# Node and segment products from split float32r operands, with the low part of x formed by VectorE

## The reference

```
neighbor_sum = segment_sum(x[col], row);  deg = max(segment_sum(1, row), 1)
mean = neighbor_sum / deg
h_mean = (x + mean) * 0.5 @ W_mean + b_mean
h_ego  = x @ W_ego + b_ego;   h_nb = mean @ W_nb + b_nb
gate = sigmoid(gw * node_vec + gb)
h = layernorm(x + (1 - gate) * h_mean + gate * concat(h_ego, h_nb))
```

## Time and profile before

| | us |
|---|---|
| median of 3 runs | 2945.29 |
| lowest and highest of them | 2940.87, 7257.4 |
| the profiled execution's own time | 2944.66 |
| its span, first to last instruction | 2942.9 |
| TensorE busy | 2697.9 |
| VectorE busy | 2329.0 |
| ScalarE busy | 1851.3 |
| GpSimd busy | 1582.4 |

### The profile page before, as it was taken

The page is one execution under the profiler, slowest core; times in us unless marked ns, Lnnn a source line. Parts: engine busy times, 40 slices in busy tenths (PEclk is TensorE's granted clock), DMA queues, the critical chain, the costliest instruction groups (busy, mean ns, idle before and its releaser), DMA issues. The chain is left out here.

```text
span 2942.9 us, 52181 instructions
## 1 busy us (share of the span) xinstructions
PE 2697.9 (92%) x13617; PEld 1554.7 (53%) x13617; DVE 2329.0 (79%) x7668; ACT 1851.3 (63%) x3839; POOL 1582.4 (54%) x1491
## 2 busy tenths in 40 slices
PE   4789889999999959999999999999999999976774
PEld 2455556666666525555555555555555555543442
DVE  8777775655565668888888888888888888878996
ACT  2344445555555437777777777777777777757885
POOL 0476717676666375455455454454554554405776
PEclk8799999999999979999999999999999999999998
DMA  9999995565555478777777787777777777647994
GB/s 339 304 301 314 306 308 182 187 192 180 182 189 189 143 182 218 215 223 214 213 227 214 213 221 216 215 218 217 219 217 212 226 213 212 193 118 241 278 278 154
DMA packets 544632, 653.46 MB, mean 222 GB/s; under 512 B 244302, under 2 KB 451850, under 8 KB 544518
## 3 DMA queue, kind: packets, MB, share of 16 engines
q1 hardware_dynamic: 468486, 440.38, 51.6%
q0 software_dynamic: 69472, 208.99, 22.7%
q10 hardware_dynamic: 6560, 2.84, 0.4%
HBM read 315.65 MB, written 299.10 MB: 209 GB/s over the span
## 5 line engine op out<-in xcount | busy, mean ns | idle before, releaser
L942 PE MATMUL bank<-w_node,xT 128*128 128x384 f32 x1564 | 568.5, 501 | 47.2 <-ACT bank L576 46.9
L1219 ACT ACTIVATE hidT<-bank,b1c 128x512 f32<-128x512 f32 x490 | 336.8, 687 | 414.5 <-PE bank L1509 340.7
L1128 POOL TENSOR_TENSOR u_hc<-u_hc 128x1536 f32<-128x1536 f32 x98 | 270.2, 2757 | 551.0 <-issue 429.0
L1509 PE MATMUL bank<-xh,w1h 128*128 128x512 f16 x1568 | 469.8, 381 | 23.1 <-DMA xh<-eh 15.7
L1509 PE MATMUL bank<-xl,w1h 128*128 128x512 f16 x1568 | 468.2, 380 | 0.0
L1509 PE MATMUL bank<-xh,w1l 128*128 128x512 f16 x1568 | 468.2, 380 | 0.0
L942 PEld LDWEIGHTS bank<-w_node,xT 128*128 128x128 f32 x1564 | 291.4, 195 | 227.7 <-ACT bank L576 61.6
L576 ACT ACTIVATE bank<-bias_all 128x512 f32<-128x512 f32 x391 | 234.3, 599 | 267.4 <-DVE H L680 266.2
L1525 PE MATMUL bank<-hidT,w2f 128*64 128x256 f32 x3136 | 360.1, 382 | 0.8 <-ACT hidT L1219 0.8
L1350 DVE STREAM_TRANSPOSE feat<-catT 32x256 f32<-32x256 f32 x784 | 342.5, 437 | 17.0 <-ACT catT L1228 2.4
L673 DVE SCALAR_TENSOR_TENSOR H<-bank,gates,X 128x256 f32<-128x256 f32 x391 | 187.2, 479 | 175.1 <-PE bank L942 172.5
(11 more groups left out here) (248 smaller groups left out, 4833.0 us busy)
## 6 DMA issues: line engine op xcount, KB each, us to landing
hc_tab<-H SPq DMA_DIRECT2D x78, 680.0 KB, 7.9
er<-edge_tab SPq DMA_DIRECT2D x98, 512.0 KB
X<-in_x SPq DMA_DIRECT2D x78, 640.0 KB, 4.8
h_row<-hc_tab SPq DMA_DIRECT2D x97, 512.0 KB
out_x<-o_row SPq DMA_DIRECT2D x97, 512.0 KB, 5.0
hc_tab<-zero_row SPq DMA_DIRECT2D x35, 1344.0 KB, 8.4
edge_tab<-u_x SPq DMA_DIRECT2D x98, 256.0 KB
edge_tab<-feat SPq DMA_DIRECT2D x98, 256.0 KB
```

Source lines behind the costliest of these rows:

```text
L942: ins = t_.matmul(p[:, 0:384], xT[t // 2 % XR][:, t % 2, c * P:(c + 1) * P], w_node[:, c, :], start=False, stop=c == 1, skip_group_check=True)
L1128: g.tensor_tensor(c, c, u_hc[s][:, :, MULT:MULT + 3].unsqueeze(3).to_broadcast([P, 4, 3, P]), ALU.mult).then_inc(u_scaled, 1)
L1219: a.activation(hidT[m][:, :], bank[2 + m % 2][:, :], ACT.Relu, bias=b1c[:, m:m + 1])\
L1509: ins = t_.matmul(bank[2 + m % 2][:, :], w[:, c, m * P:(m + 1) * P], xx[s][:, :, :].rearrange("p (k c) e -> p c k e", c=2)[:, c, :, :], st ...
```

## The change

1. `product` from the pair SPLIT = SUMS // 2 + 1 = 98 on (slot 196 and later): ScalarE copies the transposed x to `xhigh`, in float32r, VectorE subtracts that from bank 0 and gets `xlow` (`low_x`), and TensorE forms high x high, high x low and low x high with the two parts of `w_node`: six float32r matmuls in place of two fp32 ones. `xhigh` and `xlow` have two buffers each. The next `turn` waits for `x_low`.
2. `product_sum` for all pairs the same way: `accT` in float32r, `accL` by VectorE (`low_sum`, in the slot of the copy), six matmuls; the next `turn_sum` waits for `low_out`.
3. The weights are split once, by VectorE, before the loop.
4. Four x buffers in place of three, three H buffers in place of two, the store of a half is issued ahead of its clear. The clears after the fourth take 6.5 tile columns on average in place of 7, so that they end with half 40 in place of half 38.
5. SUMS 188 to 195, SPAN 186 to 177, FIX 378 to 377. `carry` is copied to a tile of its own, `carryT`.

The diff, cut to its core:

```diff
-        CLEARS = (0, 60, 88, 116) + tuple(range(144, NT, 7)) + (NT,)
+        CLEARS = (0, 60, 88, 116) + tuple(144 + 13 * c // 2 for c in range(38)) + (NT,)
...
-        XB = 3
+        XB = 4
...
+                st.done(v.tensor_copy(w_nbh[:, :, :], w_nb[:, :, :]))
+                st.done(v.tensor_copy(w_nodeh[:, :, :], w_node[:, :, :]))
+                st.wait()
+                st.done(v.tensor_tensor(w_nodel[:, :, :], w_node[:, :, :], w_nodeh[:, :, :].bitcast(F32),
+                                        ALU.subtract))
+                st.done(v.tensor_tensor(w_nbl[:, :, :], w_nb[:, :, :], w_nbh[:, :, :].bitcast(F32), ALU.subtract))
...
-        H = [tmp(f"H{s}", [P, HALF, HU]) for s in range(2)]
-        XR = 4
+        HR = 3
+        H = [tmp(f"H{r}", [P, HALF, HU]) for r in range(HR)]
+        XR = 3
...
+        XS = 2
+        xlow = [tmp(f"xlow{b}", [P, 2, D], F32R) for b in range(XS)]
+        xhigh = [tmp(f"xhigh{b}", [P, 2, D], F32R) for b in range(XS)]
...
-        SORT, PHASES, DECODE, SUMS, SPAN, FIX = 0, 7, 16, 188, 186, 378
+        SORT, PHASES, DECODE, SUMS, SPAN, FIX = 0, 7, 16, 195, 177, 377
+        SPLIT = SUMS // 2 + 1
...
+                def half(h):
+                    if h + XB <= 2 * ITER:
+                        load(h + XB)
+                    store(h)
+                    if h < len(CLEARS) - 2:
+                        clear(h + 1)
...
+                    if p >= SPLIT + XS:
+                        act.wait_ge(p_ready, 2 * (p - XS) + 2)
+                    to = xT[p % XR] if p < SPLIT else xhigh[p % XS]
+                    a.activation(to[:, 0:many, :], bank[0][:, 0:many * D].rearrange("p (t d) -> p t d", t=many),
...
+                def low_x(p):
+                    many = min(2, NT + 1 - 2 * p)
+                    dve.wait_ge(xt_copied, p + 1)
+                    if p >= SPLIT + XS:
+                        dve.wait_ge(p_ready, 2 * (p - XS) + 2)
+                    v.tensor_tensor(xlow[p % XS][:, 0:many, :],
+                                    bank[0][:, 0:many * D].rearrange("p (t d) -> p t d", t=many),
+                                    xhigh[p % XS][:, 0:many, :].bitcast(F32), ALU.subtract).then_inc(x_low, 1)
+
+                def low_sum(p):
+                    dve.wait_ge(turned_out, p + 1)
+                    if p >= AR:
+                        dve.wait_ge(prod_ready, 2 * (p - AR) + 2)
+                    v.tensor_tensor(accL[p % AR][:, :, :], bank[4][:, :].rearrange("p (t d) -> p t d", t=2),
+                                    accT[p % AR][:, :, :].bitcast(F32), ALU.subtract).then_inc(low_out, 1)
...
+                    if now % 2 == 0 and SPLIT <= (now + LEAD_X) // 2 <= NT // 2:
+                        low_x((now + LEAD_X) // 2)
+                    for p in tiles_of(now, LATE):
+                        if p < PAIRS:
+                            low_sum(p)
...
                 def turn(p):
-                    if p:
+                    if p > SPLIT:
+                        pe.wait_ge(x_low, p - SPLIT)
+                    elif p:
                         pe.wait_ge(xt_copied, p)
...
+                    if pair >= SPLIT:
+                        pe.wait_ge(x_low, pair - SPLIT + 1)
+                        high, low = xhigh[pair % XS][:, t % 2, :], xlow[pair % XS][:, t % 2, :]
+                        n = 0
+                        for c in range(2):
+                            for part_, w in ((high, w_nodeh), (high, w_nodel), (low, w_nodeh)):
+                                n += 1
+                                ins = t_.matmul(p[:, 0:384], part_[:, c * P:(c + 1) * P], w[:, c, :], start=False,
+                                                stop=n == 6, skip_group_check=True)
...
                     if p:
-                        pe.wait_ge(turned_out, p)
+                        pe.wait_ge(low_out, p)
...
+                        for part_, w in ((accT, w_nbh), (accT, w_nbl), (accL, w_nbh)):
+                            ins = t_.matmul(bank[PRODS[t % 3]][:, 0:U],
+                                            part_[t // 2 % AR][:, t % 2, c * P:(c + 1) * P], w[:, c, :],
+                                            start=n == 0, stop=n == 5)
```

More of the change, by code:

```diff
@@ L144, in build @@
         w_node = sb("w_node", [P, 2, 384])
+        w_nodeh, w_nodel = sb("w_nodeh", [P, 2, 384], F32R), sb("w_nodel", [P, 2, 384], F32R)
         w_nb = sb("w_nb", [P, 2, 384])
+        w_nbh, w_nbl = sb("w_nbh", [P, 2, 384], F32R), sb("w_nbl", [P, 2, 384], F32R)
         w1f = sb("w1f", [P, 2, HEADS * HID])
@@ L376, in build @@
         TEN = 2 * HALF
-        H = [tmp(f"H{s}", [P, HALF, HU]) for s in range(2)]
-        XR = 4
+        HR = 3
+        H = [tmp(f"H{r}", [P, HALF, HU]) for r in range(HR)]
+        XR = 3
         xT = [tmp(f"xT{b}", [P, 2, D]) for b in range(XR)]
+        XS = 2
+        xlow = [tmp(f"xlow{b}", [P, 2, D], F32R) for b in range(XS)]
+        xhigh = [tmp(f"xhigh{b}", [P, 2, D], F32R) for b in range(XS)]
+        x_low = sem("x_low")
         stats = tmp("stats", [P, TEN, 6])
@@ L383, in build @@
         sd_s = tmp("sd_s", [P, TEN])
-        h_out = [sem(f"h_out{s}") for s in range(2)]
+        h_out = [sem(f"h_out{r}") for r in range(HR)]
         o_out = [sem(f"o_out{s}") for s in range(2)]
@@ L422, in build @@
         AR = 4
-        accT = [tmp(f"accT{b}", [P, 2, D]) for b in range(AR)]
+        accT = [tmp(f"accT{b}", [P, 2, D], F32R) for b in range(AR)]
+        accL = [tmp(f"accL{b}", [P, 2, D], F32R) for b in range(AR)]
+        carryT = tmp("carryT", [P, D])
+        low_out = sem("low_out")
         carry = tmp("carry", [P, D])
@@ L475, in load, with store @@
                         sp.dma_start(X[h % XB][:, 0, :], x[N - P:N]).then_inc(x_in[h % XB], 16)
[L477 to L480, removed]
+                def store(h):
+                    sp.wait_ge(h_done, (h + 1) * HALF)
+                    sp.dma_start(h_main[:, h * HALF:(h + 1) * HALF, :], H[h % HR][:, :, :]).then_inc(h_out[h % HR], 16)
                 def clear(c):
@@ L485, in clear @@
                                  zero_row[:, :].unsqueeze(1).to_broadcast([P, hi - lo, U])).then_inc(c_zeroed, 16)
[L487 to L498, removed]
+                def half(h):
[4 more added lines that the diff above has]
+                        clear(h + 1)
+                for h in range(2 * ITER):
+                    half(h)
+                for r in range(HR):
+                    sp.wait_ge(h_out[r], 16 * len(range(r, 2 * ITER, HR)))
                 sp.wait_ge(h_done, NT + 1)
-                sp.dma_start(hc_tab[N - P:N, U:RU], H[0][:, 0, :]).then_inc(h_out[0], 16)
-                sp.wait_ge(h_out[0], 16 * ITER + 16)
+                r = 2 * ITER % HR
+                sp.dma_start(hc_tab[N - P:N, U:RU], H[r][:, 0, :]).then_inc(h_out[r], 16)
+                sp.wait_ge(h_out[r], 16 * len(range(r, 2 * ITER, HR)) + 16)
             @block.gpsimd
@@ L567, in copy_x @@
                     many = min(2, NT + 1 - 2 * p)
-                    a.activation(xT[p % XR][:, 0:many, :], bank[0][:, 0:many * D].rearrange("p (t d) -> p t d", t=many),
+                    if p >= SPLIT + XS:
+                        act.wait_ge(p_ready, 2 * (p - XS) + 2)
+                    to = xT[p % XR] if p < SPLIT else xhigh[p % XS]
+                    a.activation(to[:, 0:many, :], bank[0][:, 0:many * D].rearrange("p (t d) -> p t d", t=many),
                                  ACT.Copy).then_inc(xt_copied, 1)
@@ L631, in side @@
                         act.wait_ge(turned, PAIRS + 1)
-                        a.activation(accT[0][:, 0, :], bank[5][:, 0:D], ACT.Copy).then_inc(turned_out, 1)
+                        a.activation(carryT[:, :], bank[5][:, 0:D], ACT.Copy).then_inc(turned_out, 1)
                 def round_(j):
@@ L665, in first @@
                 def first(t, i):
-                    s, k = i // HALF, i % HALF
+                    h, k = t // HALF, t % HALF
+                    s = h % HR
                     dve.wait_ge(p_ready, t + 1)
-                    if t >= TEN and k == 0:
-                        dve.wait_ge(h_out[s], (t - i) // TEN * 16)
+                    if h >= HR and k == 0:
+                        dve.wait_ge(h_out[s], h // HR * 16)
                     if k == 0:
@@ L677, in add @@
                 def add(t, i):
-                    s, k = i // HALF, i % HALF
+                    s, k = t // HALF % HR, t % HALF
                     dve.wait_ge(a_done, t + 1)
@@ L885, in _ @@
                 hround = [0]
-                for s in range(2):
-                    v.memset(H[s][:, :, D + 3:HU], 0.0)
+                for r in range(HR):
+                    v.memset(H[r][:, :, D + 3:HU], 0.0)
                 def round_(j):
@@ L939, in product @@
                     p = bank[NODE[t % 3]]
-                    pe.wait_ge(xt_copied, t // 2 + 1)
+                    pair = t // 2
+                    if pair >= SPLIT:
[7 more added lines that the diff above has]
```

(16 more changed lines are left out.)

## The result

The changed kernel takes 2955.38 us, median of 6 runs, against 2943.79 for the kernel before: ratio 1.0038, 95% interval 1.0024 to 1.0052. It is slower, by 0.4%, where I had forecast 2890 and a range of 2868 to 2935. Its profiled execution has a span of 2954.1 us against 2942.9. Of the six runs of the kernel before, one stands apart at 7257.4 us; without it the median is 2943.73.

A forecast was written before the change was run, and what follows sets the result against it. GpSimd was to bound the second part: first scatter 448.5 + 493 + 4 = 945.5 us for the last, stage end 979 instead of 1033.4. So 2944.66 - 54.7 = 2890 us, range 2868 to 2935.

The forecast's parts named there:

- Where the time is settled: The change touches only the first stage, which ended at 1033.4 us before; later stages stay untouched.
- DMA part, 1.70 us a slot: First part of the stage: DMA bounds it at 309 GB/s, slots falling from 1.77 to 1.70 us.
- 493 + 4: First to last scatter: 493 us for 379 GpSimd scatters and gathers, plus 4 for start-up stumbles.
- float32r at one column a clock: TensorE: a float32r matmul of 384 columns takes 0.161 us, so a split product takes 0.97 instead of 1.29 us.
- Rival B: TensorE: float32r takes two columns' time, a product 1.94 us, total about 3160 us; chance 0.12.
- VectorE, 0.60 us for each low part: Each low part of x or of the sums adds 0.60 us on VectorE, making 2.58 us a slot.
- GpSimd at 1.30 us an operation as the bound, 493 us from first to last scatter: Second part: GpSimd's 379 scatters and gathers at 1.30 us bound it, 2.88 us a slot.
- the ring: Second part: copy_x waits for product(t+1), low_x for copy_x, the next turn for low_x; 5.6 us per two slots, hidden.
- Rival C: GpSimd's 1.3 us shrinks when never blocked, VectorE's 2.58 us a slot rules, total near 2825 us; chance 0.05.
- Rival D, the clock: TensorE's clock drops as gaps appear in the second part; at 20% half-speed time, total 2905 to 2950; chance 0.06.
- rival A's round: Two-slot chain through single bank 0, 5.6 us against GpSimd's 5.76; 0.5 us more gives total 2905 to 2940; chance 0.22.
- my shorter way: The two-slot chain as priced through copy_x, low_x, turn, segments and product: 5.6 us, with 0.2 for the sums' low part.

The follow-up runs named there:

- both reorderings: Changed kernel with run sums ahead of low_x and low_sum, and ScalarE's square root ahead of the copy of x, two buffers kept: 2903.11 us, ratio 0.986.

## Why the prediction was wrong

**Where the time is settled**: right. Only the first stage changed; what follows it took 1910.7 us against 1909.5.

**DMA part, 1.70 us a slot**: wrong, 1.52 measured. I took 309 GB/s at share 0.97 for the rate of the DMA engines and let the 56.8 us of store waits return at most 3%. It was the rate asked for: with the waits gone the same engines gave 342 and 361 GB/s. This error put the first scatter at 448.5 in place of 429.8. It hid part of the other, by luck: 19 us won there against 82 us lost from the first scatter to the last (579 in place of 493 + 4) leave the stage's end at 1043.4 in place of 979, the 65 us between 2890 and 2955.

**float32r at one column a clock**: right in kind. The term of 0.161 us is 0.175 measured, because I took the fp16 row's slope with no fixed part. A product is 1.05 us, not 0.97; a slot 2.68, not 2.51. Rival B, two columns' time, is out. The Trainium skill, "FP8 and Floating Point Precision", section "TensorE Precision Notes", has true FP32 in four passes. Taking a float32r matmul for one such pass, which the page doesn't say, three are three quarters of one fp32 matmul, an estimate of 0.48 us. The trace shows 0.525 against 0.646 us, 0.81: the estimate is 0.04 us short, the 0.014 us on each of three.

**VectorE, 0.60 us for each low part**: right, 0.69 and 0.68 long and 0.60 apart.

**GpSimd at 1.30 us an operation as the bound, 493 us from first to last scatter**: wrong for the changed kernel, where it is 579 us, and right for the mechanism: 500 us as soon as the ring is open, and the total then moves when half the scatters are left out. Rival C is out too: GpSimd's spacing stayed at 1.31 us.

**Rival D, the clock**: the granted clock of the second part fell to 0.97, from 1.00. By an estimate from these two numbers that is worth at most 0.03 x 450 = 14 us there. The rounds of 6.92 us ran at 1.00, so it isn't the cause, but its share of the loss was not measured.

**The step that failed is the price of rival A's round**, 5.6 us for two slots, from which I took the ring as hidden under GpSimd's 5.76. It is 6.92 where the sums fall in the even slot, and a slot is 3.36 us on average, not 2.88. I had named the ring (copy waits for the product of the next slot, low_x for the copy, turn for low_x) and given it 0.22. I had followed only the part through `turn`. The longer way goes through VectorE's program order: behind the blocked `low_x` stand `low_sum` and the two run sums, and `turn_sum` two slots on waits for those. That is 0.60 + 1.15 in place of the 0.2 I allowed for the sums, less the 0.44 that the node transposes no longer add, plus the 0.014 us on 18 matmuls, 0.25: 1.36, against 6.92 - 5.59 = 1.33 measured. The 0.25 alone would have put even my shorter way at 5.84, over 5.76; with both reorderings the trace shows 5.98 there. My instruction to myself, to ask what is queued behind a waiting instruction, I had applied on TensorE and not on VectorE, nor on ScalarE, where moving the root ahead of the copy returned another 23 us once the run sums were out of the way.

Put together from medians: rings -46 us (2943 to 2897), the segment split with the new slots and clears -30 (to 2866), the node split through two buffers +89 (to 2955). These are differences of whole kernels in that order, not parts that must add in any other.

Not settled: why seven of the 29 rounds with the sums in the odd slot, each the first after a run of even ones, took 7.5 to 9.4 us in place of 5.09.

## What to carry to other kernels

When a new wait is put on an in-order engine, follow every instruction behind it in that engine's program to whoever waits for it, up to the lag between the engines; the ring that closes through program order can be longer than the one through the data. A ring of buffers is too short when its release waits for work of a later step than the one in hand, and one more buffer (here 90 us) can be worth more than reordering (here 52 us for the two moves tried). Before taking a measured transfer rate for a limit, look whether anything waits for those transfers to land.

## What the runs showed of the hardware

- float32r matmuls of 128 x 128 weights are spaced 0.175 us at 384 columns and 0.12 at 256; an fp32 one of 384 columns is two records, 0.323 us each. Three float32r matmuls cost 0.525 us against the 0.646 of the fp32 one that they replace.
- The DMA engines gave 361 GB/s at a share of 1.05 and 342 at 1.02 in a stretch where 309 had gone with 0.97: a share near 1 was not the limit. The waits for a store to land were.
- GpSimd issues an indirect DMA of 128 rows every 1.31 us when nothing holds it, 344 in 450 us.
